# The first attention layer: from one head at a time to pairs of heads in both halves of TensorE's rows

## What is computed

```python
q, k, v = (x @ Wq, x @ Wk, x @ Wv)        # 16 heads of 16 features, x normalized
scores = einsum('bthd,bshd->bhts', q, k)
scores = scores * tril(ones((T, T)))      # masked scores are 0, not -inf
attn = softmax(scores / T ** 0.5)
out = einsum('bhts,bshd->bthd', attn, v).reshape(B, T, H * Dh) @ Wo
```

## Time and profile before

| | before |
|---|---|
| three runs | 2333.72, 2334.88, 2342.51 us |
| median | 2334.88 us |
| profiled execution, span | 2333.2 us (no other time is given for this execution; the fastest run is 0.5 us above the span) |
| TensorE busy over the span | 2060.8 us, 88% |
| VectorE, ScalarE, POOL busy | 1379.4, 954.5, 733.8 us |
| TensorE's mean granted clock | 0.931 |
| first layer | 7 to 361 us |

### The profile page before, as it was taken

One profiled execution on the slowest core, in us unless ns is written; L12 is line 12 of the kernel. 1 busy time (PEld: TensorE's weight loads), 2 busy tenths in 40 slices (PEclk: granted clock), 3 DMA queues, 4 the chain that ended last, 5 costly groups with the idle time before them and its releaser, 6 DMA issues. The chain is left out here.

```text
span 2333.2 us, 34319 instructions
## 1 busy us (share of the span) xinstructions
PE 2060.8 (88%) x11648; PEld 1608.6 (69%) x11648; DVE 1379.4 (59%) x2544; ACT 954.5 (41%) x1703; POOL 733.8 (31%) x575
## 2 busy tenths in 40 slices
PE   5999988997897565699669999999999999998798
PEld 4444436886786122588658888888888888887587
DVE  4444425447545799443667767666777677764443
ACT  2333333332432432233435555454555455553332
POOL 4111112331334775133343333223333333330232
PEclk9999997998898788799769999999999999999799
DMA  2121101221121000232100000000000000000232
GB/s 63 28 37 27 27 1 41 69 72 36 47 86 46 0 0 0 63 110 81 50 8 6 10 10 10 11 10 11 10 11 3 11 10 11 10 5 6 87 111 74
DMA packets 46195, 76.54 MB, mean 33 GB/s; under 512 B 8240, under 2 KB 28208, under 8 KB 46048
## 3 DMA queue, kind: packets, MB, share of 16 engines
q1 hardware_dynamic: 46048, 74.60, 11.1%
HBM read 64.87 MB, written 1.25 MB: 28 GB/s over the span
## 5 line engine op out<-in xcount | busy, mean ns | idle before, releaser
L337 POOL TENSOR_TENSOR f_weighted<-f_hidden,f_comb_all 128x512 f32<-128x512 f32 x128 | 190.4, 1490 | 418.3 <-DVE f_hidden L400 346.3
L791 ACT ACTIVATE gqa_probs<-acc,gqa_bias,gqa_q_scale 128x128 f32<-128x128 f32 (+7 forms) x256 | 212.6, 831 | 264.3 <-DVE gqa_bias L882 264.0
L1050 PE MATMUL aux<-gqa_probsT,gqa_v 128*128 128x128 f32 x2304 | 308.4, 280 | 1.4 <-ACT gqa_oT L813 1.4
L878 DVE TENSOR_REDUCE gqa_neg_max<-acc 128x1 f32<-128x128 f32 (+7 forms) x256 | 193.5, 756 | 173.9 <-PE acc L1017 162.8
L1050 PEld LDWEIGHTS aux<-gqa_probsT,gqa_v 128*128 128x128 f32 x2304 | 285.7, 196 | 8.2 <-issue 5.1
L734 POOL TENSOR_TENSOR gqa_q_high<-gqa_straight,gqa_turned_q 128x512 fp32r<-128x512 f32 x64 | 81.5, 1273 | 514.0 <-DVE gqa_turned_q L839 514.0
L477 PE MATMUL aux<-xnT_high,f_w_high 128*128 128x512 f32 x512 | 212.9, 416 | 23.5 <-ACT f_silu_g L358 14.0
L400 DVE TENSOR_TENSOR f_hidden<-f_silu_g,aux 128x512 f32<-128x512 f32 x128 | 87.9, 686 | 230.9 <-ACT f_silu_g L358 124.5
L477 PE MATMUL aux<-xnT_low,f_w_high 128*128 128x512 f32 x512 | 210.0, 410 | 0.0
L477 PE MATMUL aux<-xnT_high,f_w_low 128*128 128x512 f32 x512 | 209.3, 409 | 0.0
L1034 PE MATMUL aux<-ident,gqa_probs 128*128 128x128 f32 x1152 | 179.4, 280 | 7.4 <-DVE gqa_probsT L910 4.8
(11 more groups left out here) (304 smaller groups left out, 4667.1 us busy)
## 6 DMA issues: line engine op xcount, KB each, us to landing
f_comb_all<-comb_by_expert SPq DMA_DIRECT2D x48, 512.0 KB, 4.0
f_w<-in_f_up SPq DMA_DIRECT2D x64, 256.0 KB, 3.5
f_w<-in_f_down SPq DMA_DIRECT2D x64, 128.0 KB, 3.7
mat_qk<-mat_high SPq DMA_DIRECT2D x64, 64.0 KB, 2.3
mat_qk<-mat_low SPq DMA_DIRECT2D x64, 64.0 KB, 2.3
gqa_w_q<-in_g_wq SPq DMA_DIRECT2D x32, 128.0 KB, 2.1
gqa_wo<-in_g_wo SPq DMA_DIRECT2D x32, 128.0 KB, 2.1
stream<-in_x SPq DMA_DIRECT2D x1, 1024.0 KB, 5.4
```

The lines of the kernel that those rows point to most:

```text
L337: pool.tensor_tensor(weighted[:, j % SLOTS], hidden[:, j % SLOTS], comb_all[:, j // 2 % 2, j % 2 * HALF:(j % 2 + 1) * HALF], ALU.mult).the ...
L791: act.activation(probs[:, j % 4, 0:width(j)], scores(j), ACT.Exp, bias=bias[:, j % 16:j % 16 + 1], scale=q_scale[:, j // NT % 2, tile_of(j ...
L878: dve.tensor_reduce(neg_max[:, j % 16:j % 16 + 1], scores(j), AX, ALU.max, negate=True).then_inc(max_ready, 1)
L1050: last = pe.matmul(aux[:, 2 + t // 4, t % 4 * P:(t % 4 + 1) * P], v[:, g, s, :], probsT[:, j % 4, s * P:(s + 1) * P], start=(s == 0), stop ...
```

## The change

The heads are taken in pairs. Each of the two lies in one half of TensorE's rows: rows 0 to 48 and 64 to 112. A stack has three parts in place of four (high by high, high by low, low by high) and, at row 48, the row of ones against the row of maxima: 49 rows. All eight pairs have a stack of their own, which takes 96 DMAs of 64 KB; rows 49 to 63 are not used, and nothing is cleared. The ones come from two DMAs that repeat a row which POOL sets at the start.

A pair is cut into 12 query units and 12 key units, each one tile by up to 512 columns for both heads, in two PSUM banks. Three slots of two banks serve queries, keys, the turned row and the turned output in turn. Masks are added by two matmuls of 64 rows for each head. VectorE reduces a unit of both heads in one instruction, and takes one minimum more where a row's scores lie in two units. The maxima [128 x 16] of a pair are turned by one transpose, copied by ScalarE, and sent by two DMAs into the stacks' rows. The exponentials go to what were the high and low parts of the projections, eight units in a ring, so the first ones wait for all stacks. Values are multiplied in batches of four units; the four heads of two pairs lie in four groups of 32 output columns, and are turned together by eight 128 x 128 transposes. All of it is written out in one list of steps, without loops. The weight's exponential stands before the last keys.

The core of the diff (the list of steps with LAG = 6, where `key_unit` also appends a batch of values after every four keys and the turning of outputs after every 24; SP; TensorE; ScalarE):

```diff
-STACK = 4 * HD0
+PAIRS = H0 // 2
+STACK = 3 * HD0
+UNITS = 12
+        for n in range(queries):
+            steps.append(("query", n))
+            if n in (3, 7):
+                steps.append(("masked", n // 4))
+            if n % UNITS == 2 and n >= UNITS:
+                steps.append(("row", n // UNITS - 1))
+            key_unit(n - UNITS - LAG)
...
-            pool.memset(qk[STACK:P, :, :, :].bitcast(F32), 0.0).then_inc(made, 1)
-            pool.memset(qk[STACK:STACK + 1, :, 1, :].bitcast(F32), 1.0).then_inc(made, 1)
...
+            for p in range(PAIRS):
+                sp.wait_ge(low_ready, 2 if p < PAIRS // 2 else 4)
+                half = p // 4
+                for side, parts in ((0, (high, high, low)), (1, (high, low, high))):
+                    for r, part in enumerate(parts):
+                        for g in range(2):
+                            a = (2 * (p % 4) + g) * HD0
+                            sp.dma_start(rows(p, side, r)[g], part[a:a + HD0, 2 * side + half, :].bitcast(F32)).then_inc(qk_in[p], 16)
+            for p in range(PAIRS):
+                sp.wait_ge(row_ready, p + 1)
+                for g in range(2):
+                    sp.dma_start(qk[64 * g + STACK:64 * g + STACK + 1, p, 0, :].rearrange("a (t q) -> a t q", t=NT).bitcast(F32),
+                                 row[g * NT:(g + 1) * NT, p % 2, :].bitcast(F32)).then_inc(row_in[p % 2], 16)
...
+            def add_mask(s, at, mask):
+                for j in range(2):
+                    for g in range(2):
+                        rows = slice(64 * g, 64 * g + 64)
+                        last = pe.matmul(s[:, g, at:at + P], pick[rows, j, :], mask[rows, j, :], start=False, stop=j == 1)
...
+            def key(n):
+                p, b, c, lo, hi = key_unit(n)
+                free("key", n)
+                if n % UNITS == 0:
+                    pe.wait_ge(row_in[p % 2], 32 * (p // 2) + 32)
+                for g in range(2):
+                    rows = slice(64 * g, 64 * g + STACK + 1)
+                    last = pe.matmul(s[:, g, 0:hi - lo], qk[rows, p, 1, b * P:(b + 1) * P], qk[rows, p, 0, lo:hi],
+                                     start=True, stop=not masked)
...
+            def weigh(batch):
+                pe.wait_ge(exp_done, 4 * batch + 4)
+                for n in range(4 * batch, 4 * batch + 4):
+                    for g in range(2):
+                        q = 32 * (2 * (p % 2) + g)
+                        last = pe.matmul(aux[q:q + HD0 + 1, 2 + c, lo - c * HALF:hi - c * HALF], v_now[:, 2 * p + g, b, :],
+                                         probsT(n)[:, g, 0:hi - lo], start=b == 0, stop=b == 4 * c + 3, skip_group_check=True)
...
+                    if n < RING:
+                        for m in range(PAIRS):
+                            act.wait_ge(qk_in[m], 32 * LOADS)
+                    else:
+                        act.wait_ge(weighed, n - RING + 1)
+                    act.activation(probsT(n)[:, :, 0:hi - lo], slot("key", n)[:, :, 0:hi - lo], ACT.Exp, scale=SCALE).then_inc(exp_done, 1)
```

More of the change, by code:

```diff
@@ L1201, in _ @@
             sp.dma_start(wo[:, :, :], wo_dram).then_inc(wo_in, 16)
[L1203 to L1225, removed]
+            sp.wait_ge(made, 1)
@@ L1412, in _, with free @@
                     last.then_inc(v_done, 1)
-            pe.wait_ge(made, 14)
+            pe.wait_ge(made, 17)
             pe.wait_ge(low_ready, 4)
-            def sum_masked(tiles):
-                for t in tiles:
+            pe.wait_ge(v_ready, 4)
+            def free(kind, n):
+                i = place[kind, n]
+                if i < 3:
+                    return
+                was, m = slotted[i - 3]
+                if was == "query":
+                    pe.wait_ge(max_ready, m + 1)
+                elif was == "key":
+                    pe.wait_ge(exp_done, m + 1)
+                elif was == "row":
+                    pe.wait_ge(row_ready, m + 1)
+                else:
+                    pe.wait_ge(out_copied, m + 1)
@@ L1419, in sum_masked, with turn_out @@
+            def turn_out(n):
+                free("out", n)
+                pe.wait_ge(outT_copied, 2 * n + 2)
+                for t in range(NT):
+                    last = pe.transpose(flat(slot("out", n))[:, t * P:(t + 1) * P], outT_head[:, t * P:(t + 1) * P], core.ident[:, :])
+                last.then_inc(out_turned, 1)
+            def sum_masked(n):
+                for t in range(7 - 4 * n, 3 - 4 * n, -1):
                     pe.wait_ge(later_ready, NT - t)
-                    out_t = aux[:, t // 2, t % 2 * D:(t % 2 + 1) * D]
+                    if n == 1 and t % 2:
+                        pe.wait_ge(v_masked_ready, 1 if t == 3 else 2)
+                    out_t = aux[:, 2 + t // 2 % 2, t % 2 * D:(t % 2 + 1) * D]
@@ L1501, in _ @@
-            pe.wait_ge(v_ready, 4)
-            for n in range(NT):
-                score(0, n)
-                if n % 4 == 3:
-                    sum_masked(range(NT - n // 4 * 4 - 1, NT - n // 4 * 4 - 5, -1))
-            pipeline(pe, STEPS0, [(4, spread(0, 4)), (6, spread(1, 6)), (0, score), (19, turn_head), (14, score_keys), (16, weigh)],
-                     32, NT, 3 * NT)
+            for kind, n in steps:
+                if kind == "query":
+                    query(n)
+                elif kind == "masked":
+                    sum_masked(n)
+                elif kind == "row":
+                    turn_row(n)
+                elif kind == "key":
+                    key(n)
+                elif kind == "weigh":
+                    weigh(n)
+                else:
+                    turn_out(n)
```

346 lines of the change are left out of this document (170 added, 176 removed).

## The result

The changed kernel takes **2272.6 us** (median of four runs, 2271.59 to 2277.76) where the kernel before took 2335.57 on the same chip: a ratio of 0.9725, 95% interval 0.9706 to 0.9743. It is faster by 63 us; 77.9 were forecast.

What follows compares the result with a forecast made beforehand. TensorE was taken as the bound, 34.5 us for two heads. First key 96.2 + 1.5 + 144.3 of interleaved units, then the rest to 268.5 against 346.39: gain 77.9, forecast 2257 us, range 2224 to 2320.

Steps and rivals of the forecast that it cites:

- Start: Before the first query score: POOL's stack memsets go, loads start at 31.2 us, score at about 41.2; gain 8.5 us.
- SP's queue: All 96 stack loads, 0.64 us each, stand ahead of the first row of maxima: first key score at 96.2 us.
- Rival (d): The stacks' loads don't hold the keys: up to 32 us less, 2225 us; chance 0.04.
- Full overlap: TensorE, steady part: each pair of score or value matmuls costs one, 18.6 us a pair of heads before waits.
- (a): Neither packing overlaps: TensorE serializes 36.0 us a pair of heads, 2362 us, slower by 27; chance 0.12.
- (b): Only one packing overlaps: values only 2297 us (chance 0.09), scores only 2320 us (chance 0.07).
- Waits: TensorE, steady part: shared PSUM slots cost 2.6 us a pair, output transposes waiting for ScalarE 1.0; period 22.2 us.
- The clock: After TensorE's long idle time before the first key score, the clock is low at first: 1.5 us, an estimate.
- rival (c): TensorE falls to 1.2 GHz for much of the layer: time between 2257 and 2335 us; chance 0.06.
- Sum to the first normalized output: First key 96.2 + 1.5 + 144.3 interleaved, last keys and batches to 263.9, output at 268.5; gain 77.9 us.
- What follows is unchanged: Everything after the first normalized output keeps its time: profiled span 2333.2 - 77.9 = 2255.3 us.

Runs made afterwards that it cites:

- the kernel with zeros: Changed kernel plus ten matmuls of zeros ahead of every output turning, while ScalarE copies: 2258.87 us, layer end 281.0.
- the one with the early copy: Changed kernel with ScalarE copying the finished outputs after the second key of the next pair, not just before the turning: 2261.34 us, layer end 277.5.

## Why the prediction came out as it did

Direction and mechanism were right, the time 15.6 us too low; inside the range. Of the miss, 12.9 us lie in the layer up to the first normalized output, the rest behind it. By its steps:

- **Start**: right, a little high. Loads at 31.79 for 31.2, first query score at 42.52 for 41.2; the cause is shown for the large memset, and only argued for the second one.
- **SP's queue**: right, and the largest single item. First key 97.69 for 96.2: issues cost 0.66 us, not 0.64. Rival (d) falls. Sending the row early gave 31 us in the layer.
- **Full overlap**: right. From a batch's first matmul to the next score it is 3.33, 2.47 and 2.27 us at full clock, 8.07 a pair, where 7.68 + 0.66 = 8.34 were forecast. Rivals (a) and (b) fall; the values' overlap carries the gain. The Trainium skill's rule on packing (TensorE: Matmul & The Clock Gate, Packing small matmuls) gives a pack the time of one matmul and some ns more for each further one, and the trace agrees for the columns' share: two scores of 512 columns take 0.33 us together, one's 0.21 and some 0.1 as forecast for the load.
- **Waits**: right in size. The output turning waited 2.19 us for two pairs where 2 were forecast; the other waits, of 0.2 to 0.7 us, sum to 5.9 us from 155.27 to 203.12, two pairs, where 5.2 were forecast.
- **The clock**: this step failed. I charged 1.5 us once and took full clock for the rest; rival (c) took half clock throughout. It was in between. After the idle stretch the clock stayed at 0.50 until 108 us, 10 us past the first key; and in the steady part it was 0.91 to 0.95, by two dips in every two pairs, which the waits at the output turnings brought about. The period was 24.1 a pair from the first bound after the idle time to the last, where 22.2 was forecast: 11.3 us for six pairs, 2.5 of them in the first. With the waits filled, and so at a clock of 1.00, it was 22.3 over four pairs, which is the forecast: what was missing in it was the clock. The 1.5 us for the low clock at first had no row behind it, and no run isolates this cost. I had priced the fault only as a state of the whole layer, and not a dip behind each wait that I had listed myself. The Trainium skill (same page, A second HAM failure mode: psum-queue depth-cycling) says that short idle times between groups of matmuls make the clock swing; the trace agrees for the output waits of 2.19 us, while the slots' waits alone left the clock at 1.00 in the kernel with zeros and at 0.97 in the one with the early copy.
- **Sum to the first normalized output**, 268.5 forecast, 281.41 measured: +1.5 first key; +7.4 from there to the last bound (six periods +11.3, and -3.9 because the half period before the first bound has no batch of values, for which I had charged the mean, an error that by luck hid a part of the clock's cost); +4.0 from the last bound to the end. This last part isn't the clock, as the row below shows (0.98). It lies in the last key units and batches, up to the copies at 276.96: 26.0 us, where I had charged 21.9. I had taken TensorE's pace alone for them, but TensorE waits there for ScalarE's exponentials, 2.3 us in all; the other 1.8 were not traced.

```profile
250.92:276.96 26.04, 23.61 (x184) 8.79 (x179) 0.74 (x3) 12.96 (x21) 4.11 (x4) 0.98 0.00 1
```

- **"What follows is unchanged"**: not quite. 65.0 us were gained at the first normalized output and 68.9 at the first grouped-query maximum, but only 59.7 at the last one and 61.8 at the end.

Busy time over the grouped-query stage, which the change doesn't touch (columns as above), before and after:

```profile
1193.60:2127.20 933.60, 904.08 (x6095) 792.90 (x6095) 656.32 (x1505) 486.61 (x916) 286.59 (x218) 0.96 0.03 9
```

```profile
1124.70:2067.50 942.80, 911.61 (x6095) 799.19 (x6096) 659.21 (x1505) 486.40 (x916) 286.65 (x218) 0.95 0.03 8
```

The same 6095 matmuls take 9.2 us more at a slightly lower mean clock. Over the profiled executions of this study the stage took 933.6 to 943.4 us, and 936.2 in the one with zeros at the turnings, which goes with its total falling more than its layer. What sets the clock there was not found. That is why the layer's end, not the total, was compared above.

## What to carry over

When one queue carries both bulk loads and a small message that the critical path needs, count the issues ahead of the message at their measured spacing (96 at 0.66 us here) and put the message between them. Two half-height or narrow matmuls cost little more than one here, even in float32, but once they do, TensorE is no longer full and its short waits begin to cost a second time, through the clock: price such waits (2.19 us here) with the half-speed stretch behind them, and first move the wait away (12 us) before filling it with dummy work (9 us, and a loss of 4.4 where the filling was too long). And when a kernel ends a layer 2 us earlier in one execution, look whether a kernel without the edit does so too.

## What was not expected of the hardware

- TensorE did not keep program order between the two halves of its rows: by the trace's records, with a head's two masks between them, the two heads' scores still started together (at 212.94), and the reordered program took the same time. The values by heads took 5.13 us where one head after the other would take 6.4. The Trainium skill says (TensorE: Matmul & The Clock Gate, Packing small matmuls) that matmuls start in strict program order; here the records differ, for matmuls in different halves of the rows.
- Four times ten matmuls of zeros made a kernel 8.6 us faster in its layer, since the clock stayed at 1.00 where 0.91 to 0.93 had been.
- An untouched stage of 940 us took 933.6 to 943.4 us in the profiled executions of fourteen kernels, a difference of 9.8 us, more than some of the changes tried here bring.
